# The fourth quarter of a unit's turned states: scaled by ScalarE, added up by an accumulating DMA from GpSimd

## The chip, the cores and the metric

The kernel runs on one core of one Trainium2 chip. The metric is the device time of one execution in microseconds; the kernel before was run three times, and its median counts. The engines are called as in the profile: PE (TensorE, matmuls and transposes), DVE (VectorE), ACT (ScalarE), POOL (GpSimd), SP (SyncE, which here only issues DMAs).

## What is computed

A Mamba-like mixer with a post layer norm, then a feed-forward layer with a routed low-rank part and a second layer norm, for 4 sequences of 512 rows of 1024, all in float32. The change lies in the state loop of the mixer. Cut to that:

```python
proj = hidden_states @ W_in.T                 # u and gate, 2048 channels each
u = silu(conv(u) + conv_b)
dt, Bm, Cm = split(u @ Wx.T)                  # N = 16 values of Bm and Cm a row
delta = softplus(rmsnorm(dt) @ Wdt.T + dt_bias)
def step(state, xs):                          # over the 512 rows
    dA = exp(d_t[..., None] * A)
    state = dA * state + (d_t * u_t)[..., None] * B_t[:, None, :]
    y_t = einsum('bdn,bn->bd', state, C_t)    # the sum over n
    return (state, y_t)
y = (ys + u * D_param) * silu(gate)
x = layernorm(x + y @ W_out.T)
x = layernorm(x + ffn(x))
```

## The kernel before

**Units.** The state loop is cut into 256 units (b, g, n): sequence b, a group g of 4 channel tiles (512 channels), and one of the 16 state values n. A group has 16 units, so the 16 groups (0 to 15 here, in the order of time) are 4 sequences times 4. A unit has these steps:

- POOL makes the drive, delta * u times the row B of this n, for 4 tiles at once (L1563, 128x2048), in one of 3 drive buffers.
- ACT makes the decay exp(delta * A) of each tile in PSUM (L1355), 4 a unit, 3 banks.
- DVE scans each tile (L1115), 4 a unit, in place in the drive buffer.
- PE turns the states (transposes, L933): turn (s, tt) puts the quarter tt of unit s, 128 of the 512 rows by 512 channels, into one of 2 PSUM banks, state_t. It needs the unit's last scan, and the reading of the quarter two turns before.
- Each of the 4 quarters is scaled by the value of C of its row, a scalar a partition, and added to y_acc (128 x 4 x 512 in SBUF). For n = 0 ACT writes it (first, L1366). For all other n there are two ways: DVE does both in one instruction (add, L1123), or ACT scales the quarter into the buffer scaled (L1375) and POOL adds that to y_acc (sum, L1568).

Behind n = 15 PE turns the sum back (y_turn), and DVE (y_skip) and POOL (y_gate) finish it. Beside this chain PE works off the products: the in products of the next sequence with weights split in a high and a low part (u_mm, g_mm, lines L964 to L966; the low part is made by POOL, w_low, L1588), the out products of this or the last one (o_mm, L987), and the feed-forward ones.

**What sets the order.** A planner (class Plan) plays the kernel through with a cost for each piece, and starts on each free engine the ready piece that is due first; every engine then runs its list in that order, with semaphore waits. put() gives a piece its engine, due time, cost, needs, and the buffers it takes and gives back. The two ways of a quarter are rivals there (either): whichever the planner can start first is done and the other struck out. The way over ACT is allowed only when POOL is free within FREE_IN = 3 us and has no work due more than DUE_EARLIER earlier. It chose the DVE way 727 times and the other 233 times: 8 times in group 0, 15 in group 1, and 12 to 18 in each later one, on any of the quarters (94 times the first, 26 the second, 82 the third, 31 the fourth). There is one scaled buffer, and there are 4 scratch buffers, which gates, copies and other rows share.

```python
put("DVE", i + 5 - ADD_FIRST, 0.645, "add", (s, tt), [*turned, summed(s - 1, tt)])
put("ACT", i + 5 - ADD_FIRST, 0.575, "scale", (s, tt), turned, take=[("scaled", (s, tt))], ahead_of="POOL")
put("POOL", q + 4, 1.23, "sum", (s, tt), [("scale", (s, tt)), summed(s - 1, tt)], give=[("scaled", (s, tt))])
plan.either(("add", (s, tt)), ("scale", (s, tt)))
```

Of the kernel before, what the change touches and what calls it, by code (L numbers as in the profile page):

```python
# [7 lines left out]
ALU = mybir.AluOpType  # L8
ACT = mybir.ActivationFunctionType
AX = mybir.AxisListType  # L10

P = 128
# [33 lines left out]
BANKS, SCRATCH, RAW, SPLIT = 3, 4, 4, 4  # L46
# [12 lines left out]
FREE_IN, DUE_EARLIER = 3, 8  # L59

def added(s, tt):

    if UNITS[s][2] == 0:
        return [(("first", (s, tt)), ("first", (s, tt)))]
    return [(("add", (s, tt)), ("add", (s, tt))), (("scale", (s, tt)), ("sum", (s, tt)))]
# [15 lines left out]
def any_of(names):  # L82
    return tuple(names) if len(names) > 1 else names[0]

def turn_read(s, tt):
    return any_of([read for read, _ in added(s, tt)])

def summed(s, tt):  # L90
    return any_of([end for _, end in added(s, tt)])
# [14 lines left out]
class Plan:  # L106
# [11 lines left out]
    DELAY = {"PE": 0.25, "DVE": 0.13, "ACT": 0.13, "POOL": 0.15, "SP": 2.0}  # L118

    def __init__(self):  # L120
        self.pieces, self.work = {}, {e: [] for e in ENGINES}
        self.count, self.total = {}, {}
        self.pools = {"bank": BANKS, "scratch": SCRATCH, "raw": RAW, "split": SPLIT, "dt": 1, "scaled": 1}
        self.place, self.before, self.prior, self.rival = {}, {}, {}, {}
        self.weights = []

    def put(self, engine, due, us, stage, key, needs=(), take=(), give=(), spare=0, kb=0, ahead_of=None):
# [5 lines left out]
                                       give=list(give), spare=spare, kb=kb, order=len(self.pieces), ahead_of=ahead_of)  # L133

    def either(self, add, scale):

        self.rival[add], self.rival[scale] = (scale, 2), (add, 1)

    def done_way(self, names):

        return next(name for name in ([names] if names in self.pieces else names) if name in self.count)

    def arrange(self):
# [6 lines left out]
        for name, piece in self.pieces.items():  # L150
            for need in set(piece["needs"]):
                left[name] += 1
                for way in [need] if need in self.pieces else need:
                    then[way].append(name)
# [12 lines left out]
        while finished < wanted:  # L167
            for e in ENGINES:
                for entry in sorted(ready[e]) if at[e] <= now else []:
# [4 lines left out]
                    on = piece["ahead_of"]  # L174
                    if on and (at[on] > now + FREE_IN or any(due < entry[0] - DUE_EARLIER for due, _, _ in ready[on])):
                        continue
                    ready[e].remove(entry)
                    if entry[2] in self.rival:
                        lost, pieces = self.rival[entry[2]]
                        wanted -= pieces  # L180
                        for other in ENGINES:
                            ready[other] = [x for x in ready[other] if x[2] != lost]
# [13 lines left out]
                    end = at[e] + self.DELAY[e]  # L196
# [28 lines left out]
def make_plan():  # L225
# [327 lines left out]
    for s, (b, g, n) in enumerate(UNITS):  # L553
# [13 lines left out]
        put("POOL", q - 8, 4.56 if s else 2.35, "drive", s, [("fetch", s), ("du", (b, g, 1))] + ([] if s else [("drive_begun", 0)]) + (  # L567
# [8 lines left out]
        for tt in range(TT):  # L576
            i = TT * s + tt
            turned = [("turn", (s, tt)), ("ssm_norm", b)]
            put("PE", i + 4 - TURN_FIRST, 0.45, "turn", (s, tt), [("scan", (s, GT - 1)), *([] if i else [("ssm_norm", 0)])] + (
# [1084 lines left out]
```

## Time and profile before

| | |
|---|---|
| Runs, us | 2257.61, 2262.97, 2263.51 (median 2262.97) |
| Span of the profiled execution, us | 2257.2 |
| Units of the state loop run, us from the start | 142 to 2136 |
| Mean granted PE clock, as a share of the full one | 0.964 |
| PE, DVE, POOL, ACT busy in the span | 91%, 88%, 81%, 66% |

The span goes from the first instruction's start to the last one's end. A time of the table's first row is of a whole execution; the lowest, 2257.61, is 0.4 us over the span of the profiled one. The busy time of an engine is the union of its instructions' times; an idle stretch ahead of an instruction is put down to what ended it. DVE's instructions overlap by about 0.08 us when one follows the other, so the distance of two starts is what one costs, not the duration. Group k starts with unit 16 k; the first scans of groups 2 and 12 stand at 426.0 and 1669.7 us.

### The profile page before, as it was taken

The page shows a single profiled execution, that of the slowest core. Times are in us where ns is not written, and L with a number is a line of the kernel's source. Part 1 is how long each engine was busy: PE and PEld are TensorE (multiplying, and loading weights), DVE is VectorE, ACT ScalarE, POOL GpSimd, SP SyncE. Part 2 cuts the span into 40 slices and gives each one's busy share as a digit, 9 for nine tenths or more (in the row PEclk, how much of TensorE's full clock was granted, in tenths as well). Part 3 has the DMA queues.
Part 4 walks back from the last instruction along what each step waited for, and adds up shares of the span by engine and source line. Part 5 has one row for each costly group of instructions (what it writes and reads, how often), then busy time and mean ns, then how long its engine had stood idle before and what let it go on. Part 6 is the DMA issues. An engine that isn't in the chain of part 4 may idle for free. (4 is left out here: it accounts for less than half of the span.)

```text
span 2257.2 us, 30761 instructions
## 1 busy us (share of the span) xinstructions
PE 2063.3 (91%) x10528; PEld 1562.5 (69%) x10528; DVE 1986.4 (88%) x2398; ACT 1486.3 (66%) x2198; POOL 1824.8 (81%) x786
## 2 busy tenths in 40 slices
PE   8989789889999799799998997989999998897998
PEld 6867577778565478687875555867875556785677
DVE  4447779999999999899999999999999999999943
ACT  4478658787666677666886657676786667756531
POOL 4279899998898889768799997979788998698840
PEclk9989899999999999999999998999999999998999
DMA  4466566665333447655463432475463337443340
GB/s 157 138 223 235 204 221 219 203 205 179 92 118 86 126 132 239 209 193 182 158 199 95 111 96 96 147 264 171 143 203 101 110 96 233 148 144 132 101 143 38
DMA packets 168764, 354.84 MB, mean 157 GB/s; under 512 B 18656, under 2 KB 45408, under 8 KB 168608
## 3 DMA queue, kind: packets, MB, share of 16 engines
q1 hardware_dynamic: 168608, 352.87, 48.6%
q8 instruction: 84, 1.38, 0.2%
q14 instruction: 72, 0.59, 0.1%
HBM read 283.96 MB, written 68.85 MB: 156 GB/s over the span
## 5 line engine op out<-in xcount | busy, mean ns | idle before, releaser
L1563 POOL TENSOR_TENSOR drive<-delta_u,b_bcast 128x2048 f32<-128x2048 f32 (+1 forms) x257 | 1172.5, 4564 | 129.1 <-PE state_t L933 120.6
L1115 DVE TENSOR_TENSOR_SCAN drive<-decay,drive 128x512 f32<-128x512 f32 x1024 | 1190.5, 1203 | 62.0 <-POOL drive L1563 37.9
L1355 ACT ACTIVATE decay<-delta,a_sb 128x512 f32<-128x512 f32 x1024 | 694.7, 688 | 377.9 <-DVE drive L1115 374.6
L933 PEld LDWEIGHTS state_t<-identity,drive 128*128 128x128 f32 x4096 | 492.0, 146 | 311.1 <-DVE drive L1115 141.8
L933 PE MATMUL state_t<-identity,drive 128*128 128x128 f32 x4096 | 591.1, 284 | 119.8 <-DVE drive L1115 95.1
L1123 DVE SCALAR_TENSOR_TENSOR y_acc<-state_t,c_rows,y_acc 128x512 f32<-128x512 f32 x727 | 515.3, 734 | 54.3 <-PE state_t L933 51.7
L964 PE MATMUL bank<-cols_high,w_split 128*128 128x512 f32 (+1 forms) x1240 | 524.4, 423 | 26.6 <-POOL w_split L1588 11.8
L966 PE MATMUL bank<-cols_high,w_split 128*128 128x512 f32 (+1 forms) x1240 | 491.8, 397 | 0.0
L965 PE MATMUL bank<-cols_low,w_split 128*128 128x512 f32 (+1 forms) x1240 | 489.6, 395 | 0.0
L987 PE MATMUL bank<-channels,w_raw 128*128 128x512 f32 x896 | 420.2, 596 | 2.3 <-DVE rows L1177 2.0
L1568 POOL TENSOR_TENSOR y_acc<-y_acc,scaled 128x512 f32<-128x512 f32 x233 | 300.1, 1288 | 102.2 <-ACT scaled L1375 101.9
L964 PEld LDWEIGHTS bank<-cols_high,w_split 128*128 128x128 f32 (+1 forms) x1240 | 236.3, 191 | 71.9 <-issue 16.2
L966 PEld LDWEIGHTS bank<-cols_high,w_split 128*128 128x128 f32 (+1 forms) x1240 | 234.8, 189 | 54.5 <-issue 0.2
L965 PEld LDWEIGHTS bank<-cols_low,w_split 128*128 128x128 f32 (+1 forms) x1240 | 237.1, 191 | 38.7 <-issue 0.5
L1588 POOL TENSOR_TENSOR w_split<-w_raw,w_split 128x512 fp32r<-128x512 f32 (+1 forms) x130 | 165.7, 1283 | 110.6 <-ACT w_split L1396 110.5
L987 PEld LDWEIGHTS bank<-channels,w_raw 128*128 128x128 f32 x896 | 156.4, 192 | 123.8 <-issue 121.3
L1375 ACT ACTIVATE scaled<-state_t,c_rows 128x512 f32<-128x512 f32 x233 | 159.2, 683 | 109.1 <-PE state_t L933 81.9
L1130 DVE SCALAR_TENSOR_TENSOR channels<-bank,conv_w_sb,channels 128x511 f32<-128x511 f32 (+2 forms) x192 | 142.7, 744 | 48.0 <-ACT channels L1404 43.5
L1396 ACT ACTIVATE w_split<-w_raw 128x512 fp32r<-128x512 f32 (+1 forms) x130 | 80.5, 621 | 58.9 <-PE bank L966 16.4
L1355 ACT ACT_TABLE_LOAD x80 | 102.6, 1283 | 2.0 <-DVE drive L1115 0.6
L1584 POOL TENSOR_TENSOR channels<-channels,scratch 128x512 f32<-128x512 f32 x64 | 81.5, 1296 | 12.3 <-DVE channels L1167 12.3
L1577 POOL TENSOR_TENSOR delta_u<-delta,channels 128x512 f32<-128x512 f32 x64 | 80.8, 1293 | 5.9 <-ACT delta L1458 5.5
(204 smaller groups left out, 1451.8 us busy)
## 6 DMA issues: line engine op xcount, KB each, us to landing
w_split<-w_split SPq DMA_DIRECT2D x272, 512.0 KB, 4.0
b_bcast<-b_rows SPq DMA_DIRECT2D x256, 256.0 KB, 3.4
w_raw<-in_w_out SPq DMA_DIRECT2D x112, 256.0 KB, 3.0
w_raw<-in_w_in SPq DMA_DIRECT2D x96, 256.0 KB, 4.1
gates<-scratch SPq DMA_DIRECT2D x64, 256.0 KB, 3.7
scratch<-gates SPq DMA_DIRECT2D x64, 256.0 KB, 4.7
rows<-in_x_rows SPq DMA_DIRECT2D x4, 2048.0 KB, 8.2
out<-rows SPq DMA_DIRECT2D x16, 512.0 KB, 4.8
```

Of the source, the lines that this page charges most:

```text
L933: last = engine.transpose(bank[0:tile.shape[1], i * P:(i + 1) * P], tile, identity[:, :])
L964: engine.matmul(bank[:, :], high[:, k % WK, :], cols_high[:, k, :], start=first, stop=False)
L965: engine.matmul(bank[:, :], high[:, k % WK, :], cols_low[:, k, :], start=False, stop=False)
L966: engine.matmul(bank[:, :], low[:, k % WK, :], cols_high[:, k, :], start=False, stop=last).then_inc(signal[stage])
L987: engine.matmul(bank[:, :], tile[:, k % WK, :], chan[s % 2][:, k, :], start=(k == tiles[0]), stop=(k == tiles[-1])).then_inc(signal["o_mm"])
L1115: engine.tensor_tensor_scan(state, decay[(GT * s + t) % DECAYS][:, :], state, 0.0, ALU.mult, ALU.add).then_inc(signal["scan"])
L1123: engine.scalar_tensor_tensor(y_acc[:, tt, :], bank[:, :], c, y_acc[:, tt, :], ALU.mult, ALU.add).then_inc(signal["add"])
L1355: engine.activation(decay[i % DECAYS][:, :], delta[:, g % 2, t, :], ACT.Exp, scale=a_sb[:, j, n:n + 1]).then_inc(signal["decay"])
L1375: engine.activation(scaled[:, :], bank[:, :], ACT.Copy, scale=c_rows[b % 2][:, tt, n:n + 1]).then_inc(signal["scale"])
L1563: engine.tensor_tensor(drive[key % DRIVES][:, tiles, :], du[:, tiles, :], row, ALU.mult).then_inc(signal[stage])
L1568: engine.tensor_tensor(y_acc[:, tt, :], y_acc[:, tt, :], scaled[:, :], ALU.add).then_inc(signal["sum"])
L1588: engine.tensor_tensor(pair[:, 1, 0:cols], raw[place["raw", key]][:, 0:cols], pair[:, 0, 0:cols].bitcast(F32), ALU.subtract).then_inc(sign ...
```

## The change

The choice between the two ways is fixed. The rivals, FREE_IN, DUE_EARLIER and ahead_of are gone from the planner. For the units with n from 1 to 14 the fourth quarter (tt = 3, BY_DMA) is scaled by ACT into one of 2 scaled buffers and added to y_acc by a DMA with accumulation, 128 x 512 float32 (256 KB), that POOL issues on its own queue; the planner counts 1.0 us for the issue and 4.0 us until it has landed. The three other quarters, and all four of n = 15, are DVE's adds. POOL waits, before it issues the DMA of a unit, until the DMA of the unit before has landed (both change the same rows of y_acc); the fourth add of n = 15 waits on DVE for the landing of n = 14. SCRATCH goes from 4 to 3. turn now waits for all four scans, drive for the drive before. The space for descriptors of DMAs issued by GpSimd goes from 64 to 512.

```diff
-BANKS, SCRATCH, RAW, SPLIT = 3, 4, 4, 4
+BANKS, SCRATCH, RAW, SPLIT, SCALED = 3, 3, 4, 4, 2
...
-FREE_IN, DUE_EARLIER = 3, 8
...
+BY_DMA = range(TT - 1, TT)
+
+
+def by_dma(s, tt):
+
+    return 0 < UNITS[s][2] < N - 1 and tt in BY_DMA
...
+    return "first" if UNITS[s][2] == 0 else "scale" if by_dma(s, tt) else "add", (s, tt)
...
+    return ("sum", s) if by_dma(s, tt) else turn_read(s, tt)
...
+    DMA_SUM = 4.0
...
-            put("DVE", i + 5 - ADD_FIRST, 0.645, "add", (s, tt), [*turned, summed(s - 1, tt)])
-            put("ACT", i + 5 - ADD_FIRST, 0.575, "scale", (s, tt), turned, take=[("scaled", (s, tt))], ahead_of="POOL")
-            put("POOL", q + 4, 1.23, "sum", (s, tt), [("scale", (s, tt)), summed(s - 1, tt)], give=[("scaled", (s, tt))])
-            plan.either(("add", (s, tt)), ("scale", (s, tt)))
+            if by_dma(s, tt):
+                put("ACT", i + 5 - ADD_FIRST, 0.575, "scale", (s, tt), turned, take=[("scaled", s)] if tt == BY_DMA[0] else [])
+            else:
+                put("DVE", i + 5 - ADD_FIRST, 0.645, "add", (s, tt), [*turned, summed(s - 1, tt)])
+        if by_dma(s, BY_DMA[0]):
+            put("POOL", q + 8, 1.0, "sum", s, [x for tt in BY_DMA for x in (("scale", (s, tt)), summed(s - 1, tt))], give=[("scaled", s)])
...
                 elif stage == "sum":
-                    s, tt = key
-                    e.wait_ge(*done("scale", key))
-                    e.wait_ge(*in_sum(s - 1, tt))
-                    engine.tensor_tensor(y_acc[:, tt, :], y_acc[:, tt, :], scaled[:, :], ALU.add).then_inc(signal["sum"])
+                    i = place["scaled", key]
+                    for tt in BY_DMA:
+                        e.wait_ge(*done("scale", (key, tt)))
+                        e.wait_ge(*in_sum(key - 1, tt))
+                    engine.dma_start(y_acc[:, BY_DMA[0]:BY_DMA[-1] + 1, :], scaled[i][:, :, :], accum_op=ALU.add).then_inc(sum_landed[i], 16)
...
-    nc = bacc.Bacc("TRN2", target_bir_lowering=False, num_devices=1, dynamic_dma_scratch_size=64)
+    nc = bacc.Bacc("TRN2", target_bir_lowering=False, num_devices=1, dynamic_dma_scratch_size=512)
```

The planner now makes another order on every engine. Adds and split quarters by group, from the two orders: before, 8 and 15 quarters went over ACT in groups 0 and 1 and 210 in groups 2 to 15; now 14 in every group.

POOL, from the drive of unit 188 on to the first drives of group 12 (unit 192 is drive0 behind the delta_u rows). Before:

```order
L1563 TENSOR_TENSOR drive2<-delta_u,b_bcast0 128x2048
L1568 TENSOR_TENSOR y_acc<-y_acc,scaled 128x512
L1563 TENSOR_TENSOR drive0<-delta_u,b_bcast1 128x2048
L1563 TENSOR_TENSOR drive1<-delta_u,b_bcast0 128x2048
L1568 TENSOR_TENSOR y_acc<-y_acc,scaled 128x512
L1563 TENSOR_TENSOR drive2<-delta_u,b_bcast1 128x2048
L1568 TENSOR_TENSOR y_acc<-y_acc,scaled 128x512
L1577 TENSOR_TENSOR delta_u<-delta,channels1 128x512 x4
L1563 TENSOR_TENSOR drive0<-delta_u,b_bcast0 128x2048
L1568 TENSOR_TENSOR y_acc<-y_acc,scaled 128x512
L1563 TENSOR_TENSOR drive1<-delta_u,b_bcast1 128x2048
```

and of the change (there L1554 is the drive, L1569 delta_u, L1560 the accumulating DMA):

```order
L1554 TENSOR_TENSOR drive2<-delta_u,b_bcast0 128x2048
L1560 DMA y_acc<-scaled0 128x512
L1554 TENSOR_TENSOR drive0<-delta_u,b_bcast1 128x2048
L1560 DMA y_acc<-scaled1 128x512
L1554 TENSOR_TENSOR drive1<-delta_u,b_bcast0 128x2048
L1560 DMA y_acc<-scaled0 128x512
L1554 TENSOR_TENSOR drive2<-delta_u,b_bcast1 128x2048
L1560 DMA y_acc<-scaled1 128x512
L1569 TENSOR_TENSOR delta_u<-delta,channels1 128x512 x4
L1560 DMA y_acc<-scaled0 128x512
L1554 TENSOR_TENSOR drive0<-delta_u,b_bcast0 128x2048
L1560 DMA y_acc<-scaled1 128x512
```

Where a sum stood at a place or not, by the planner's choice, a DMA stands behind each drive; the one behind drive0 is that of n = 14 of group 11, for which the fourth add of n = 15 waits.

DVE, in the same place: from the scans of unit 191 (drive2, n = 15) to those of unit 192 (drive0). The scans read a decay bank, the adds state_t0 (quarters 1 and 3) or state_t1 (2 and 4). Before:

```order
L1115 SCALAR_TENSOR_TENSOR drive2<-decay2,drive2 128x512
L1115 SCALAR_TENSOR_TENSOR drive2<-decay0,drive2 128x512
L1123 SCALAR_TENSOR_TENSOR y_acc<-state_t1,c_rows0,y_acc 128x512
L1115 SCALAR_TENSOR_TENSOR drive2<-decay1,drive2 128x512
L1123 SCALAR_TENSOR_TENSOR y_acc<-state_t0,c_rows0,y_acc 128x512
L1123 SCALAR_TENSOR_TENSOR y_acc<-state_t1,c_rows0,y_acc 128x512
L1115 SCALAR_TENSOR_TENSOR drive2<-decay2,drive2 128x512
L1115 SCALAR_TENSOR_TENSOR drive0<-decay0,drive0 128x512
L1115 SCALAR_TENSOR_TENSOR drive0<-decay1,drive0 128x512
L1123 SCALAR_TENSOR_TENSOR y_acc<-state_t0,c_rows0,y_acc 128x512
```

and of the change (L1106 the scan, L1114 the add), from the scan of unit 191's last tile on:

```order
L1106 SCALAR_TENSOR_TENSOR drive2<-decay2,drive2 128x512
L1106 SCALAR_TENSOR_TENSOR drive0<-decay0,drive0 128x512
L1114 SCALAR_TENSOR_TENSOR y_acc<-state_t0,c_rows0,y_acc 128x512
L1114 SCALAR_TENSOR_TENSOR y_acc<-state_t1,c_rows0,y_acc 128x512
L1106 SCALAR_TENSOR_TENSOR drive0<-decay1,drive0 128x512
L1114 SCALAR_TENSOR_TENSOR y_acc<-state_t0,c_rows0,y_acc 128x512
L1106 SCALAR_TENSOR_TENSOR drive0<-decay2,drive0 128x512
L1114 SCALAR_TENSOR_TENSOR y_acc<-state_t1,c_rows0,y_acc 128x512
L1106 SCALAR_TENSOR_TENSOR drive0<-decay0,drive0 128x512
```

Unit 191 has all its adds on DVE both times; the fourth one (the last L1114) now stands behind the third scan of unit 192. In the units before it, the quarter that leaves DVE was any one and is now always the fourth.

## Rows read from the trace of the kernel before

**Rows 1.** Page, parts 1 and 3: busy time, share, instructions; DMA packets, MB, share

```profile
PE 2063.3 (91%) x10528; PEld 1562.5 (69%) x10528; DVE 1986.4 (88%) x2398; ACT 1486.3 (66%) x2198; POOL 1824.8 (81%) x786
...
q1 hardware_dynamic: 168608, 352.87, 48.6%
```

**Rows 2.** Stretch, us; busy PE, PEld, DVE, ACT, POOL (instructions), clock, DMA share, GB/s

```profile
142.00:426.00 284.00, 248.40 (x1270) 200.16 (x1268) 234.56 (x258) 211.95 (x313) 261.54 (x122) 0.95 0.65 224
426.00:2136.00 1710.00, 1580.17 (x8184) 1170.84 (x8184) 1646.58 (x1957) 1176.24 (x1728) 1471.12 (x593) 0.97 0.48 151
```

**Rows 3.** Waits in 426 to 2136 us: us in total, times, longest

```profile
POOL drive L1563 <- PE state_t L933: 117.9, 81, 8.4
...
POOL y_acc L1568 <- ACT scaled L1375: 101.9, 66, 5.1
...
DVE y_acc L1123 <- PE state_t L933: 32.7, 45, 2.8
ACT scaled L1375 <- POOL y_acc L1568: 25.0, 29, 2.3
...
DVE drive L1115 <- ACT decay L1355: 18.6, 16, 3.1
...
PE state_t L933 <- ACT scaled L1375: 6.9, 11, 1.7
```

**Rows 4.** Waits in 142 to 426 us

```profile
DVE drive L1115 <- POOL drive L1563: 36.7, 11, 13.6
...
POOL w_split L1588 <- ACT w_split L1396: 14.8, 9, 3.9
```

**Rows 5.** Timeline of DVE: start, us, instruction, [idle before]

```profile
683.86 1.60 DVE L1123 SCALAR_TENSOR_TENSOR y_acc<-state_t,c_rows,y_acc 128x512 f32<-128x512 f32 x2 [1.21 <-PE state_t L933]
...
990.52 1.41 DVE L1123 SCALAR_TENSOR_TENSOR y_acc<-state_t,c_rows,y_acc 128x512 f32<-128x512 f32 x2 [1.24 <-PE state_t L933]
...
1673.27 1.21 DVE L1115 TENSOR_TENSOR_SCAN drive<-decay,drive 128x512 f32<-128x512 f32 x1
...
2023.47 0.72 DVE L1123 SCALAR_TENSOR_TENSOR y_acc<-state_t,c_rows,y_acc 128x512 f32<-128x512 f32 x1
2024.11 1.21 DVE L1115 TENSOR_TENSOR_SCAN drive<-decay,drive 128x512 f32<-128x512 f32 x1
...
2136.97 0.75 DVE L1123 SCALAR_TENSOR_TENSOR y_acc<-state_t,c_rows,y_acc 128x512 f32<-128x512 f32 x1 [0.75 <-PE state_t L933]
```

**Rows 6.** Groups of DVE in 426 to 2136 us: busy, mean ns, idle before

```profile
L1123 DVE SCALAR_TENSOR_TENSOR y_acc<-state_t,c_rows,y_acc 128x512 f32<-128x512 f32 x629 | 445.3, 733 | 34.8 <-PE state_t L933 32.7
```

**Rows 7.** Page, part 5: groups of POOL

```profile
L1563 POOL TENSOR_TENSOR drive<-delta_u,b_bcast 128x2048 f32<-128x2048 f32 (+1 forms) x257 | 1172.5, 4564 | 129.1 <-PE state_t L933 120.6
...
L1568 POOL TENSOR_TENSOR y_acc<-y_acc,scaled 128x512 f32<-128x512 f32 x233 | 300.1, 1288 | 102.2 <-ACT scaled L1375 101.9
```

**Rows 8.** Page, part 6: DMA issues, KB each, us to landing

```profile
w_split<-w_split SPq DMA_DIRECT2D x272, 512.0 KB, 4.0
...
gates<-scratch SPq DMA_DIRECT2D x64, 256.0 KB, 3.7
scratch<-gates SPq DMA_DIRECT2D x64, 256.0 KB, 4.7
```

**Rows 9.** Timeline of SP: one issue

```profile
1008.66 0.32 SPq L886 DMA_DIRECT2D b_bcast<-b_rows  x1
```

**Rows 10.** Timeline of POOL: first drives of groups 12 and 15

```profile
1665.07 4.61 POOL L1563 TENSOR_TENSOR drive<-delta_u,b_bcast 128x2048 f32<-128x2048 f32 x1
...
2013.29 4.65 POOL L1563 TENSOR_TENSOR drive<-delta_u,b_bcast 128x2048 f32<-128x2048 f32 x1
```

**Rows 11.** Busy us in a stretch of out products

```profile
570.00:627.00 57.00, 57.00 (x244) 32.92 (x243) 56.93 (x64) 32.48 (x51) 50.04 (x19) 1.00 0.35 96
```

**Rows 12.** Timeline of ACT ahead of a late decay

```profile
1370.26 4.62 ACT L1471 ACTIVATE rows<-rows,ln_shift,ln_rstd 128x1024 f32<-128x1024 f32 x4
1374.79 1.29 ACT L1355 ACTIVATE decay<-delta,a_sb 128x512 f32<-128x512 f32 x2
```

More of the change, by code:

```diff
@@ L122, in __init__, with put @@
         self.count, self.total = {}, {}
-        self.pools = {"bank": BANKS, "scratch": SCRATCH, "raw": RAW, "split": SPLIT, "dt": 1, "scaled": 1}
-        self.place, self.before, self.prior, self.rival = {}, {}, {}, {}
+        self.pools = {"bank": BANKS, "scratch": SCRATCH, "raw": RAW, "split": SPLIT, "dt": 1, "scaled": SCALED}
+        self.place, self.before, self.prior = {}, {}, {}
         self.weights = []
-    def put(self, engine, due, us, stage, key, needs=(), take=(), give=(), spare=0, kb=0, ahead_of=None):
+    def put(self, engine, due, us, stage, key, needs=(), take=(), give=(), spare=0, kb=0):
         assert (stage, key) not in self.pieces, (stage, key)
         self.pieces[stage, key] = dict(engine=engine, due=due, us=us, name=(stage, key), needs=list(needs), take=list(take),
[L133 to L141, printed above, removed]
+                                       give=list(give), spare=spare, kb=kb, order=len(self.pieces))
     def arrange(self):
@@ L152, in arrange @@
                 left[name] += 1
-                for way in [need] if need in self.pieces else need:
-                    then[way].append(name)
+                then[need].append(name)
             for what in piece["give"]:
@@ L641, in build_mixer_ffn @@
         scratch = [sbuf(f"scratch{i}", [P, T]) for i in range(SCRATCH)]
-        scaled = sbuf("scaled", [P, GT * P])
+        scaled = [sbuf(f"scaled{i}", [P, len(BY_DMA), GT * P]) for i in range(SCALED)]
         identity = sbuf("identity", [P, P])
@@ L762, in build_mixer_ffn @@
             landed[stage, key] = (to, raised[id(to)])
+        for _, stage, key in plan.work["POOL"]:
+            if stage == "sum":
+                to = sum_landed[place["scaled", key]]
+                raised[id(to)] = raised.get(id(to), 0) + 16
+                landed[stage, key] = (to, raised[id(to)])
         def read(s, tt):
-            return done(*plan.done_way(turn_read(s, tt)))
+            return done(*turn_read(s, tt))
         def in_sum(s, tt):
-            return done(*plan.done_way(summed(s, tt)))
+            return done(*summed(s, tt))
         def x_first(k):
@@ L940, in _ @@
                     s, tt = key
-                    e.wait_ge(*done("scan", (s, GT - 1)))
+                    for t in range(GT):
+                        e.wait_ge(*done("scan", (s, t)))
                     i = TT * s + tt
@@ L1369, in _ @@
                     b, g, n = UNITS[s]
[L1370 removed]
+                    bank, to, prior = state_banks[(TT * s + tt) % TURNED], scaled[place["scaled", s]], before["scaled", s]
                     e.wait_ge(*done("turn", key))
@@ L1374, in _ @@
                         e.wait_ge(*done(*prior))
-                    engine.activation(scaled[:, :], bank[:, :], ACT.Copy, scale=c_rows[b % 2][:, tt, n:n + 1]).then_inc(signal["scale"])
+                    engine.activation(to[:, tt - BY_DMA[0], :], bank[:, :], ACT.Copy, scale=c_rows[b % 2][:, tt, n:n + 1]).then_inc(signal["scale"])
                 elif stage == "x_high":
```

26 lines of the change are left out of this document (5 added, 21 removed).

## The prediction, made before the changed kernel was run

> **What bounds the kernel now.** I read the busy table first, then three stretches. Over the span PE is busy 91%, DVE 88%, POOL 81%, ACT 66% [rows 1], an average over stages with different limits. The second view splits it [rows 2]. In 426 to 2136 us, which holds groups 2 to 15 of the state loop, DVE is busy 1646.6 of 1710 us, so it stands idle for 63.4; PE is busy 1580.2, POOL 1471.1, ACT 1176.2. In 142 to 426 us (groups 0 and 1) the fullest engine is POOL, 261.5 of 284, and DVE has 234.6. The tail behind 2136 us has none of the work that the change touches. So DVE paces most of the kernel, PE close behind it, and POOL paces the start.
>
> The waits say the same. In the middle stretch DVE waits for PE's turns 32.7 us, for ACT's decays 18.6, and for POOL's drives only 1.2; POOL itself waits 117.9 us for turns before it may write a drive, that is, it runs ahead [rows 3]. In groups 0 and 1 DVE waits 36.7 us for POOL's drives [rows 4]. A reader should look there before the page's totals: taking 300 us off POOL is worth nothing in a stretch where nobody waits for POOL.
>
> **What the change takes from each engine.** Before, 727 adds are DVE's and 233 are split between ACT (scale) and POOL (sum). After, the split ones are the fourth quarter of units with n 1 to 14, 14 in each of 16 groups: 224. DVE has 736.
>
> *DVE.* Where the nine come from matters. By the order, groups 0 and 1 held 23 split adds and now hold 28; groups 2 to 15 held 210 and now hold 196. So in the stretch where DVE paces, it gains 14 adds. An add lasts 733 ns [rows 6], but neighbours overlap: two take 1.41 us, and a scan behind an add starts 0.64 after it [rows 5]; over the stretch I take 0.655 for one. 14 x 0.655 = **+9.2 us**. The 5 that DVE loses in groups 0 and 1 fall where it waits for POOL anyway: 0.
>
> *DVE's waits for turns.* A first add directly behind the unit's last scan must wait, since PE cannot turn before the scan ends: about 1.2 us each. In groups 2 to 15 the order has 12 such places, 14.5 us in all (the first at 683.86, one at 990.52, the last at 2136.97 [rows 5]); the new order has 17: 5 x 1.2 = +6.0. Against that, adds of the fourth quarter, and third-quarter adds behind a split one, now carry almost none of the rest of the 32.7 us; summed over the 629 adds of the stretch by what stands ahead of each, they carried about 9, and the new order keeps 2 of it. 6 - 7 = **-1 us**.
>
> *ACT.* Nine scales less, on an engine with 534 us idle in the middle stretch [rows 2]: 0.
>
> *POOL.* 233 sums at 1.288 us go (300.1 us [rows 7]), 224 DMA issues come. No row shows what GpSimd pays to issue one. The lower bound is SP's: 0.32 us an issue [rows 9]. The upper one is the drive, 4.56 [rows 7], the longest thing POOL does here. I take 1.1, since the instruction touches the same 128 rows as the sum at 1.29 does, without passing the data. In the middle stretch POOL has 239 us idle and gives back 271.7 for 196 issues, so it becomes the bound only if an issue costs over (239 + 272) / 196 = 2.6 us; 0 at 1.1. In groups 0 and 1 POOL paces: the order has 20 sums before the drive of unit 32, and the new one 27 issues, the other pieces being equal in number: 27 x 1.1 - 20 x 1.29 = 3.9, of which I count half, because POOL also stands 14.8 us for ACT there [rows 4]: **+2 us**. With 0.32 it would be -17 at full weight, with 2.6 +44.
>
> *The landing.* The new wait: POOL's issue for unit s waits until the DMA of unit s - 1 has landed, with later drives queued behind it; and at a group's end the fourth add of n = 15 waits on DVE for the landing of n = 14, with all later scans behind it, and PE's y_turn too. Mid-group a unit lasts about 7.6 us (1710 / 224), and a drive (4.6) stands between two issues, so a landing within some 6 us of its issue costs nothing. At the group's end the order puts the DMA behind the next group's first drive. In the trace such a drive ends at 1669.68 and 2017.94 [rows 10]. The third scan behind it ends at 1674.48 and the third add of its unit would follow, 5.4 us after the drive; at the other end the fourth add starts at 2023.47, 5.5 after it [rows 5]. Counted in the same way, nine of the fifteen ends have a margin between 4.3 and 6 us, the others up to 11. Transfers of 256 KB land in 3.7 to 4.7 us, of 512 KB in 4.0 [rows 8]; an accumulating one reads its target too. I take 4.1 behind an issue of 1.1, so 5.2: **+2 us** (9 x 0.2). Lower end 3.7, nothing; upper end 9 us, about twice the slowest median, below as a rival.
>
> The Trainium skill ("DMA: Bandwidth & Descriptors", anatomy of one DMA) gives about 2.0 us plus bytes / 436e3 for a DMA issued from GpSimd, 2.6 us here as an estimate. No row here shows such a DMA; the 256 KB rows are all longer. By that page the ends would cost nothing and the sum would be 2 us less.
>
> *The rest.* turn waits for all four scans instead of the last, drive for the drive before: DVE and POOL run in order, so 0. SCRATCH falls from 4 to 3, which could hold back PE's gate and out products; by the order PE has at least as much product work done by each group's start as before from unit 32 on, within 3 of about 5264 pieces where it is behind. 0, if DMAs land as they do now (stores of gates 3.7, loads 4.7 [rows 8]). More traffic: 224 x 0.26 MB is 59 MB on 353 [rows 1], so DMA share in the middle 0.48 [rows 2] becomes about 0.56, 0.64 if the second read counts fully.
>
> **The sum.** 9.2 - 1 + 2 + 2 = **+12 us**. The profiled execution has a span of 2257.2, and the run at 2257.61 is the one nearest to it; the other two are at 2263, and the median is 2262.97. So 2270 for an execution like the profiled one, and **2275** for the median.
>
> **Rivals.**
> 1. *The landing takes over* (slower still). One mechanism: accumulation makes the DMA long. From 5 us after the issue begins each further us costs about 9 us at the nine tight ends, from 6 on all fifteen, and from about 7.6, one unit, POOL's queue runs at the DMA's pace. At 8 us: 9 x 3 + 6 x 2 = 39 at the ends, over 2300. For: two reads and one write of 2 KB rows. Against: 512 KB lands in 4.0 [rows 8]. A milder form is contention.
> The Trainium skill (same page, "Issuing engines are not separate DMA queues") says DMAs of all issuing engines run on the same 16 DMA engines and interleave. By it the extra 59 MB also lengthens the weight loads; the DMA share, 0.65 in groups 0 and 1 against 0.48 later, says where that would begin. Its worth is in this case's 12%.
> 2. *The adds hide* (no change). In stretches of out products PE is busy 57.00 of 57 us with DVE at 56.93 [rows 11]. Groups 8 to 11 lie partly in such stretches, and 12 of the 14 adds fall in them. If it is PE that paces there, they go into DVE's 63 us of idle time: 9 us less, 2266 at the median, within 0.3%.
> 3. *Faster, by the banks.* Before, ACT's scale waits 25.0 us for POOL to free the one scaled buffer (29 times), POOL waits 101.9 us for scales with drives queued behind, and PE waits 6.9 us for ACT to free a state bank [rows 3]. With two buffers and a quarter that nobody on DVE follows, these go. If ACT's late decays (18.6 on DVE) came of them, and PE paces, the change gives back 6.9 + 18.6 and removes the 9.2: 2263 - 25 + 4 = about 2242; with half of it 2254. Against: a late decay such as that at 1374.79 stands behind four norms of 4.62 us, not behind a scale [rows 12]. It shows as faster once more than 11 of the 25 us are real.
> 4. *The change doesn't do what it says*: if POOL waits at the issue until the data has moved, an issue costs 3.7 or more [rows 8], over the 2.6 at which POOL paces: 2263 + 196 x 1.1 = above 2400. 2%, within the 12% of case 1.
>
> **The numbers.** Forecast 45% (own range 2266 to 2284), landing 12%, hidden 23%, faster 20%. A measurement of this kernel tells about 0.3%, 7 us, from no change. Of the forecast's 45 I count 39 as slower and 6 as same; of the hidden case 20 same, 3 faster; of the faster case 18 faster, 2 same; the landing case is slower. Faster 0.21, same 0.28, slower 0.51. The range leaves out half of the faster case and most of the landing case: 2249 to 2300.
>
> **What the new profile would show.** DVE's adds x736 at about 733 ns, DVE idle in the middle stretch still near 63 us and the stretch about 10 us longer: the forecast. DVE waiting at the group ends for a DMA, and PE's bank turns late there: rival 1. POOL's DMA rows over 2.6 us: rival 4. DVE idle well below 63 and the span unchanged: rival 2. ACT's scale without waits, DVE's wait for decays near zero and a shorter middle: rival 3. The forecast fails if POOL's issues are near 0.3 us, since then groups 0 and 1 gain up to 17 us, or if DVE's idle time moves by more than 10 us for reasons of order that a count of places does not catch.

## The result and the profile after

The changed kernel takes **2312.12 us** (median of 4 runs, 2305.58 to 2313.84), the kernel before 2263.24 beside it: a ratio of **1.0218, interval 1.0199 to 1.0238**, or 49 us slower. The forecast was 2275, with a range of 2249 to 2300: the sign was right and the size was not. The profiled executions have spans of 2310.4 and 2257.2 us.

First the page of the kernel after: busy time (to be held against [rows 1]), DMA queues, the chain that ended last, the groups of POOL ([rows 7]) and the landings ([rows 8]).

```profile
PE 2089.4 (90%) x10528; PEld 1573.2 (68%) x10528; DVE 1994.9 (86%) x2407; ACT 1479.6 (64%) x2189; POOL 1729.5 (75%) x777
...
q1 hardware_dynamic: 168608, 352.87, 47.5%
q0 software_dynamic: 32256, 58.73, 14.4%
...
PE 45%; DVE 23%; issue 9%; POOL 8%; ACT 7%; DMA 6%; SPq 0%; DVEq 0%; POOLq 0%; ACTq 0%
...
L1554 POOL TENSOR_TENSOR drive<-delta_u,b_bcast 128x2048 f32<-128x2048 f32 (+1 forms) x257 | 1201.2, 4690 | 269.4 <-PE state_t L923 255.4
...
L1560 POOL DMA_DIRECT2D y_acc<-scaled x224 | 207.8, 928 | 102.9 <-DMA y_acc<-scaled 63.0
...
L1580 POOL TENSOR_TENSOR w_split<-w_raw,w_split 128x512 fp32r<-128x512 f32 (+1 forms) x130 | 178.7, 1406 | 116.5 <-ACT w_split L1387 116.5
...
w_split<-w_split SPq DMA_DIRECT2D x272, 512.0 KB, 4.6
...
y_acc<-scaled POOLq DMA_DIRECT2D x224, 256.0 KB, 5.3
```

POOL has 95 us less work, as it should, and stands 63.0 us waiting for landings. Its drives, which nobody touched, have grown from 4564 to 4690 ns, and SP's 512 KB loads land in 4.6 us where they took 4.0. The DMA to y_acc is now 6% of the chain that ended last.

Then the stretches, with the columns of [rows 2]: the two that answer to it are groups 0 and 1, and groups 2 to 15.

```profile
143.00:437.00 294.00, 256.93 (x1285) 206.24 (x1284) 230.70 (x250) 216.52 (x320) 259.02 (x130) 0.93 0.77 241
437.00:2193.00 1756.00, 1601.31 (x8180) 1178.32 (x8179) 1660.11 (x1972) 1167.23 (x1716) 1383.28 (x581) 0.96 0.63 177
```

Groups 0 and 1 went from 284 to 294 us, groups 2 to 15 from 1710 to 1756. In the second stretch DVE's work grew by 13.5 us (1646.6 to 1660.1) and its idle time by 32.5 (63.4 to 95.9). The forecast had 9.2 of work there and 1 us of waits. The waits of that stretch, to be held against [rows 3] (us in total, times, longest):

```profile
POOL drive L1554 <- PE state_t L923: 248.6, 122, 7.1
...
ACT scaled L1366 <- PE state_t L923: 118.2, 78, 4.4
...
POOL y_acc L1560 <- DMA y_acc<-scaled: 51.3, 30, 4.9
DVE y_acc L1114 <- PE state_t L923: 36.3, 49, 2.9
DVE drive L1106 <- ACT decay L1346: 31.7, 27, 3.6
...
DVE y_acc L1114 <- DMA y_acc<-scaled: 7.3, 6, 2.5
...
DVE drive L1106 <- POOL drive L1554: 6.2, 4, 2.1
```

DVE's idle time grew in four places: decays 18.6 to 31.7, landings 0 to 7.3, POOL's drives 1.2 to 6.2, turns 32.7 to 36.3. That is 29.0 of the 32.5 us. Only one of the four names the DMA. How the DMA can reach DVE by way of another wait can be watched at one group end. POOL's timeline there (start, us, instruction, idle before):

```profile
1698.06 0.93 POOL L1560 DMA_DIRECT2D y_acc<-scaled  x1
...
1706.04 0.88 POOL L1560 DMA_DIRECT2D y_acc<-scaled  x1 [2.01 <-DMA y_acc<-scaled]
1706.64 4.91 POOL L1554 TENSOR_TENSOR drive<-delta_u,b_bcast 128x2048 f32<-128x2048 f32 x1
1713.00 0.90 POOL L1560 DMA_DIRECT2D y_acc<-scaled  x1 [1.45 <-DMA y_acc<-scaled]
```

and DVE's:

```profile
1711.58 1.22 DVE L1106 TENSOR_TENSOR_SCAN drive<-decay,drive 128x512 f32<-128x512 f32 x1 [1.24 <-POOL drive L1554]
...
1719.48 0.75 DVE L1114 SCALAR_TENSOR_TENSOR y_acc<-state_t,c_rows,y_acc 128x512 f32<-128x512 f32 x1 [2.47 <-DMA y_acc<-scaled]
```

POOL stands 2.01 us at 1706.04, until the DMA issued at 1698.06 has landed. The drive queued behind the issue starts that much later and ends at 1711.55, and DVE's scan, which stood 1.24 us, starts then. The next issue waits 1.45 us again, for the DMA issued at 1706.04, so that one took 7.0 us. The last one is issued at 1713.00 and holds DVE's fourth add until 1719.48, 6.5 us later. Three landings in a row hold this chain (8.0, 7.0 and 6.5 us behind their issues), and DVE pays at two places, 1.24 us for a drive and 2.47 for the landing itself.

### The profile page after: what moved, and what is told of

Same layout as the page of the kernel before. It is cut to its first block, busy times and chain, and to the rows that moved or that the text cites. A ratio compares the mean times of both kernels' runs of the same rounds, so it can differ in the third digit from the quotient of the medians.

```text
span 2310.4 us, 31004 instructions
## 1 busy us (share of the span) xinstructions
PE 2089.4 (90%) x10528; PEld 1573.2 (68%) x10528; DVE 1994.9 (86%) x2407; ACT 1479.6 (64%) x2189; POOL 1729.5 (75%) x777
## 3 DMA queue, kind: packets, MB, share of 16 engines
q0 software_dynamic: 32256, 58.73, 14.4%
## 4 chain that ended last, share of the span: by engine, by line
PE 45%; DVE 23%; issue 9%; POOL 8%; ACT 7%; DMA 6%; SPq 0%; DVEq 0%; POOLq 0%; ACTq 0%
DVE drive L1106 12%; PE bank L978 10%; PE state_t L923 10%; DVE y_acc L1114 6%; DMA y_acc<-scaled 6%; PE bank L955 5%; PE bank L957 5%; PE bank L956 5%; POOL drive L1554 5%; DVE channels L1121 2%; PE bank L923 2%; PE bank L1023 2%; POOL w_split L1580 1%; ACT decay L1346 1%; ACT L1346 1%
## 5 line engine op out<-in xcount | busy, mean ns | idle before, releaser
L1554 POOL TENSOR_TENSOR drive<-delta_u,b_bcast 128x2048 f32<-128x2048 f32 (+1 forms) x257 | 1201.2, 4690 | 269.4 <-PE state_t L923 255.4
L1106 DVE TENSOR_TENSOR_SCAN drive<-decay,drive 128x512 f32<-128x512 f32 x1024 | 1195.5, 1205 | 76.2 <-POOL drive L1554 38.3
L1114 DVE SCALAR_TENSOR_TENSOR y_acc<-state_t,c_rows,y_acc 128x512 f32<-128x512 f32 x736 | 523.1, 735 | 84.7 <-PE state_t L923 73.2
L955 PEld LDWEIGHTS bank<-cols_high,w_split 128*128 128x128 f32 (+1 forms) x1240 | 238.6, 192 | 75.1 <-issue 15.5
L1560 POOL DMA_DIRECT2D y_acc<-scaled x224 | 207.8, 928 | 102.9 <-DMA y_acc<-scaled 63.0
L957 PEld LDWEIGHTS bank<-cols_high,w_split 128*128 128x128 f32 (+1 forms) x1240 | 237.3, 191 | 55.5
L1580 POOL TENSOR_TENSOR w_split<-w_raw,w_split 128x512 fp32r<-128x512 f32 (+1 forms) x130 | 178.7, 1406 | 116.5 <-ACT w_split L1387 116.5
L1366 ACT ACTIVATE scaled<-state_t,c_rows 128x512 f32<-128x512 f32 x224 | 152.2, 679 | 136.7 <-PE state_t L923 123.4
L1569 POOL TENSOR_TENSOR delta_u<-delta,channels 128x512 f32<-128x512 f32 x64 | 85.9, 1577 | 5.6 <-ACT delta L1449 5.5
```

The source lines that it names most:

```text
L955: engine.matmul(bank[:, :], high[:, k % WK, :], cols_high[:, k, :], start=first, stop=False)
L957: engine.matmul(bank[:, :], low[:, k % WK, :], cols_high[:, k, :], start=False, stop=last).then_inc(signal[stage])
L1106: engine.tensor_tensor_scan(state, decay[(GT * s + t) % DECAYS][:, :], state, 0.0, ALU.mult, ALU.add).then_inc(signal["scan"])
L1114: engine.scalar_tensor_tensor(y_acc[:, tt, :], bank[:, :], c, y_acc[:, tt, :], ALU.mult, ALU.add).then_inc(signal["add"])
L1554: engine.tensor_tensor(drive[key % DRIVES][:, tiles, :], du[:, tiles, :], row, ALU.mult).then_inc(signal[stage])
L1560: engine.dma_start(y_acc[:, BY_DMA[0]:BY_DMA[-1] + 1, :], scaled[i][:, :, :], accum_op=ALU.add).then_inc(sum_landed[i], 16)
```

## The experiments

The theory after this profile: of the 49 us, part is the order that the new plan lays down, whatever carries out the sum, and part is the accumulating DMA. The rivals: the landing waits carry all of it; or the traffic does. Each ratio is to the kernel before, run beside it on the same chip.

**Who sums, in the same order.** Three kernels keep the changed order on every engine. The first lets POOL sum as it did before, the second leaves the fourth quarters' sums out, the third lets the DMA copy over y_acc in place of adding. The edits, shortened:

```diff
-engine.dma_start(y_acc[...], scaled[i][:, :, :], accum_op=ALU.add)
+engine.tensor_tensor(y_acc[:, TT - 1, :], y_acc[:, TT - 1, :], scaled[i][:, 0, :], ALU.add)   (e1)
+(nothing)                                                                              (e2)
+engine.dma_start(y_acc[...], scaled[i][:, :, :])                                       (e3)
```

> The changed kernel with one thing put back: POOL adds the scaled quarter to y_acc by its own instruction, at the place in its list where the DMA is issued. The order on all five engines is that of the changed kernel. Theory L (the landing costs: median 5.3 us from issue, 63 us of waits on POOL, 7 on DVE): the sum is done 1.3 us after it starts, the landing waits go, POOL's drives are back at 4.56 us; 2275, that is within 6 us of +12 over before. Theory O (the new order itself costs, whoever adds): it stays within 7 us of the changed kernel, 2305 to 2319.

> The changed kernel without the sum: POOL neither adds nor issues, so the fourth quarters of n 1 to 14 are left out of y_acc; ACT still scales them, and who waited for the sum waits for the scale. All other lists are the same. It is the floor for this order: Theory L: 2265 to 2275 (DVE has 14 adds more in groups 2 to 15 than before, and no landing). Theory O: 2300 or more. If it is under 2263, the sum's place on POOL matters more than DVE's adds.

> The changed kernel with a DMA that overwrites y_acc's fourth quarter in place of adding to it (the sum over n is lost for that quarter); same bytes written, same issue, same waits. It tells the price of accumulating. If the second read of the target makes the landing long: landing falls from 5.3 to about 4.2 us, POOL's waits for it from 63 to under 20, and the time to about 2290. If it is the path over GpSimd and not the accumulation: landing 5 us or more and 2305 to 2315.

Measured: e1 2288.58 us, ratio 1.0131 (1.0114 to 1.0148); e2 2277.19, 1.0082 (1.0067 to 1.0097); e3 2280.35, 1.0097 (1.0082 to 1.0113). So the changed kernel costs 18.6 us over the one before with no sum in it at all; nine more adds on DVE and the scratch buffer are in that number, beside the order itself. A plain copy adds 3 more, which these intervals do not tell from nothing, and accumulating adds 27 to that. POOL's own sum at the DMA's place (e1) costs 11 more than no sum and 8 more than the plain copy, so e1 lies between its two theories, 30 us over before, and the DMA costs 20 us more than the sum it stands for. e2 came out 2 us above the range of theory L, and e3 10 us under its 2290. POOL's groups and the landing in e3, the plain copy:

```profile
L1554 POOL TENSOR_TENSOR drive<-delta_u,b_bcast 128x2048 f32<-128x2048 f32 (+1 forms) x257 | 1170.1, 4554 | 340.0 <-PE state_t L923 319.3 <-DMA b_bcast<-b_rows 15.0 <-DMA y_acc<-scaled 3.6
...
L1560 POOL DMA_DIRECT2D y_acc<-scaled x224 | 129.9, 580 | 56.3 <-ACT scaled L1366 33.4 <-DMA y_acc<-scaled 15.2 <-PE state_t L923 5.8
...
q0 software_dynamic: 17920, 58.73, 6.6%
...
y_acc<-scaled POOLq DMA_DIRECT2D x224, 256.0 KB, 4.3
```

The same bytes need 80 packets a DMA and not 144, and 6.6% of the DMA engines' time and not 14.4%. They land in 4.3 us and not 5.3, are issued in 0.58 and not 0.93, and leave the drive at 4554 ns.

**The fixed choice by itself.** Here POOL sums again, and the planner is told so (1.23 us and POOL's own delay), with the choice fixed as in the change.

```diff
-put("POOL", q + 8, 1.0, "sum", s, ...)      end = ... DMA_SUM if stage == "sum"
+put("POOL", q + 4, 1.23, "sum", s, ...)     end = ... DELAY[e]
```

> The fixed choice with the sum on POOL and the planner told so (1.23 us, due as before, no landing of 4 us), so the order is made anew. It is the change without its DMA. Theory L: 2263 to 2275, the 14 adds of DVE in groups 2 to 15 being all that is left (9 us). Theory O in the form that a fixed choice is bad whatever follows: 2290 or more.

Measured: 2271.65 us, 1.0054 (1.0037 to 1.0072). Fixed choice, nine more adds and SCRATCH 3 together: 12 us, within the range of theory L. The kernel before with only the number SCRATCH set to 3:

> The kernel before with one number changed, SCRATCH 3 for 4, the planner's choice kept. It asks what the scratch buffer costs that the change gives up. If the buffer is not missed (as the prediction put it at 0): within 4 us of before. If it is part of the 18.6 us that the changed order costs even without any sum: 5 us slower or more.

2262.64 us, 1.0012 (1.0002 to 1.0022): 3 us. This is not the price of the buffer at equal work: with one buffer fewer the planner also chose the way over ACT 250 times and not 233, so DVE has 710 adds and not 727.

The order laid out for the DMA costs 6 us over one laid out for POOL when nobody sums (e2 against e4), and 17 when POOL sums in both (e1 against e4). The 6 do not lie in groups 2 to 15, which take 1734 us in e2 and 1732 in e4, but in groups 0 and 1, 285 against 276. What the order changes in groups 2 to 15 is for whom DVE waits. Its waits for decays there are 18.6 us before, 17.0 in e4, 27.8 in e2, 31.7 in the change. Two of the long ones, at the same places of the order: this is the timeline of DVE in e2,

```profile
531.44 3.59 DVE L1104 TENSOR_TENSOR_SCAN drive<-decay,drive 128x512 f32<-128x512 f32 x3 [3.57 <-ACT decay L1344]
1085.12 3.59 DVE L1104 TENSOR_TENSOR_SCAN drive<-decay,drive 128x512 f32<-128x512 f32 x3 [2.92 <-ACT decay L1344]
```

and this in the change, where the same scans wait as long:

```profile
542.35 3.59 DVE L1106 TENSOR_TENSOR_SCAN drive<-decay,drive 128x512 f32<-128x512 f32 x3 [3.57 <-ACT decay L1346]
...
1102.38 3.59 DVE L1106 TENSOR_TENSOR_SCAN drive<-decay,drive 128x512 f32<-128x512 f32 x3 [2.91 <-ACT decay L1346]
```

**Is it the wait or the work?** In e7 the DMA accumulates the scaled tile onto itself, so nobody needs its landing, except the scale that fills the slot again. The fourth quarters' sums are left out.

```diff
-engine.dma_start(y_acc[...], scaled[i][:, :, :], accum_op=ALU.add)
+engine.dma_start(scaled[i][:, :, :], scaled[i][:, :, :], accum_op=ALU.add)
```

> The order of the changed kernel; the accumulating DMA is issued as there, but from the scaled buffer onto itself, so y_acc misses the fourth quarters of n 1 to 14, and nobody waits for its landing except ACT, before it uses that buffer again two units later. It keeps the issue, the traffic and the work on POOL and takes the waits away. If the waits on the landing make the 27 us over the plain copy: 2278 to 2284, near the run without a sum. If it is what the accumulating DMA does to others while it runs (POOL's drives at 4.69 instead of 4.56 us, issues at 0.93 instead of 0.58, weights landing later): 2295 or more.

Measured: 2298.06 us, 1.0170 (1.0155 to 1.0185). That is 11 us less than the change; 16 us over the plain copy stay although POOL and DVE wait for no landing. The drive takes 4711 ns. But the waits for landings have not gone without a successor. A wait that is 3.0 us in the whole change, "issue", is 46.4 us here: POOL stands before the DMA with no semaphore to wait for.

```profile
POOL scaled L1561 <- issue: 46.4, 37, 3.7
```

```profile
300.05 1.00 POOL L1561 DMA_DIRECT2D scaled<-scaled  x1
300.66 5.05 POOL L1555 TENSOR_TENSOR drive<-delta_u,b_bcast 128x2048 f32<-128x2048 f32 x1
309.44 0.90 POOL L1561 DMA_DIRECT2D scaled<-scaled  x1 [3.73 <-issue]
```

Two reasons were open: the space for the DMA's descriptors is full, or the earlier DMA itself holds POOL. e9 is e7 with `dynamic_dma_scratch_size` 1024 in place of 512.

> As e7_dma_unwaited (accumulating DMA onto its own scaled tile, nobody waits for its landing but the next use of the slot, y_acc leaves out the fourth quarters), same order on every engine, only the space for POOL's DMA descriptors is doubled from 512 to 1024. In e7 POOL stood 46.4 us in 37 places before an issue with no semaphore to wait for, and the ratio was 1.017. Theory A, the space is full while the earlier accumulate is in flight: these 46 us go, and the time comes down from 2298 to 2280-2288. Theory B, the previous accumulating DMA or the engine itself holds the issue: the stalls stay at 35-55 us and the time within 4 us of 2298.

Measured: 2292.38 us, 1.0138 (1.0117 to 1.0158). The same place in e9:

```profile
300.02 0.76 POOL L1561 DMA_DIRECT2D scaled<-scaled  x1
300.63 4.79 POOL L1555 TENSOR_TENSOR drive<-delta_u,b_bcast 128x2048 f32<-128x2048 f32 x1
305.20 1.07 POOL L1561 DMA_DIRECT2D scaled<-scaled  x1
305.81 5.11 POOL L1555 TENSOR_TENSOR drive<-delta_u,b_bcast 128x2048 f32<-128x2048 f32 x1
```

**Bytes or number?** e12 is the change in its exact order, but a DMA covers 256 of the 512 columns; the other half of the fourth quarter's sum is left out.

```diff
-engine.dma_start(y_acc[:, BY_DMA[0]:BY_DMA[-1] + 1, :], scaled[i][:, :, :], ...)
+engine.dma_start(y_acc[:, TT - 1, 0:GT * P // 2], scaled[i][:, 0, 0:GT * P // 2], ...)
```

> The change in its exact order, but each accumulating DMA covers only the first half of the 512 columns (128 KB in place of 256 KB); the other half of the fourth quarter's sum is left out. Theory A, the cost of accumulating goes with bytes and packets in flight: landing 5.3 to 3.8-4.3 us, POOL's wait for landing 63 to under 20 us, drive 4.69 to 4.60 us, and the time is 2288-2296. Theory B, the cost goes with the issue or the mere number of accumulating DMAs: issue stays at 0.93 us, drive at 4.69, and the time stays at 2303-2312.

Measured: 2287.41 us, 1.0121 (1.0103 to 1.0139). Its POOL groups and DMA rows:

```profile
L1554 POOL TENSOR_TENSOR drive<-delta_u,b_bcast 128x2048 f32<-128x2048 f32 (+1 forms) x257 | 1201.5, 4693 | 282.6 <-PE state_t L923 266.1 <-DMA b_bcast<-b_rows 12.8 <-DMA y_acc<-scaled 3.2
L1560 POOL DMA_DIRECT2D y_acc<-scaled x224 | 210.2, 938 | 63.7 <-ACT scaled L1366 28.4 <-DMA y_acc<-scaled 22.6 <-PE state_t L923 8.5
...
q0 software_dynamic: 32256, 29.37, 8.3%
...
y_acc<-scaled POOLq DMA_DIRECT2D x224, 128.0 KB, 4.5
```

Both theories are half right, and the rows part them. The packets are as many as before, and so the issue (938 ns) and the drive (4693) stay. The landing falls from 5.3 to 4.5, POOL's wait for it from 63.0 to 22.6, and the time by 22 us. So what falls with the bytes is worth 22 us of the 49; the slower POOL and what else is left of the DMA cost the rest above e2, 9 us, and above the plain copy, whose drives are not slowed, 5.

**Would a plan that knows the landing help?** DMA_SUM is 4.0 us in the plan; the trace says 5.3 from issue start.

> The changed kernel with the planner told 7 us from issue to landing instead of 4, so that the fourth adds at the group ends and the issues stand later. If the landing costs because the plan counts on 4 us and gets 5.3 in the median and 7.3 in one of ten: 2285 to 2300, a good part of the 27 us between it and the plain copy comes back. If the cost is the wait itself (a drive queued behind on POOL, the whole group end held back): 2305 or more, and the ends get longer by what the plan adds.

> The change with DMA_SUM = 5.0 in place of 4.0 in its plan, near the measured landing of 5.3 us. Theory A, from e6_planned_7us (ratio 1.152, every unit 140-158 us per group): the planner can't place an issue of 1 us + landing behind a 4.56 us drive within one unit's 7.6 us, so the plan itself stretches; the plan's own length goes from 2257.7 to 2343 us, and the run adds about 50 us as in e6: 2380-2400. Theory B, the plan at 7.0 was a case by itself and a truer landing helps: the waits of 63 us on POOL fall under 30 and the time is 2290-2305.

Measured: with 7.0, 2604.87 us, 1.1520 (1.1500 to 1.1539); with 5.0, 2389.22, 1.0564 (1.0545 to 1.0584). The first is 300 us above the nearest number that its expectation named; "2305 or more" covers it by the letter only, for neither theory had a plan that stretches every unit. A theory of stretched plans made from that miss gave 2380 to 2400 for the second, and met it. The landing is as before (5.2 and 5.3 us); it is the order that spreads. DVE's waits in e11:

```profile
DVE y_acc L1114 <- PE state_t L923: 117.2, 110, 3.2
...
POOL y_acc L1560 <- DMA y_acc<-scaled: 57.5, 30, 5.2
...
DVE drive L1106 <- POOL drive L1554: 46.0, 29, 13.6
```

A planner that fills one engine at a time puts the issue (1.0), the landing (5.0) and a drive (4.56) that may have just begun in a row. That is 10.6 us on a chain with a pitch of 7.6, so it spaces units out in the plan, and the fixed order then keeps that spacing on the chip. That the chain is this one is my reading, and it is not complete: with 4.0 the same sum is 9.6, over the pitch too, and the plan spreads far less. That the spacing is the plan's is shown, since only the number in the plan differs.

**More for POOL instead.** e8 is e4 with n = 15 split too (240 sums, 720 adds on DVE):

> The replanned kernel with the sum on POOL, but n from 1 to 15 split instead of 1 to 14: 16 adds fewer on DVE (720), 240 sums on POOL. It tests the price of one add on the pacing engine: 16 x 0.655 = 10.5 us less than with 14 a group, if DVE paces, so about 2261, even with before, which has 727 adds. If other waits take it back: 2268 to 2275.

Measured: 2279.47 us, 1.0084 (1.0066 to 1.0101), 18 us above what was expected. DVE's idle time in groups 2 to 15 grew by 9.5 us over e4 and groups 0 and 1 by 10.3 (286.8 us, where e4 has 276.5 and the kernel before 284). A new order by itself moves the time by some 10 us, and a small saving in work can drown in it.

e10 keeps the choice of the kernel before and gives it a second scaled tile (the three settings, before and in e10):

```diff
-BANKS, SCRATCH, RAW, SPLIT = 3, 4, 4, 4        FREE_IN, DUE_EARLIER = 3, 8        "scaled": 1
+BANKS, SCRATCH, RAW, SPLIT = 3, 3, 4, 4        FREE_IN, DUE_EARLIER = 1, 8        "scaled": 2
```

> The kernel before, choice kept, with two scaled tiles in place of one (SCRATCH 3 to make room) and the planner's leeway for a scale set to 1 us in place of 3. POOL then sums 304 places in place of 233, DVE adds 71 fewer. Theory (my rival 3, ScalarE's 25 us of waiting for the one scaled tile is worth something): the wait ACT scaled<-POOL falls under 8 us, and the plan's own length, 12 us shorter than before's, comes through: 2244-2252, faster than both kernels. Rival: POOL, with 71 sums of 1.29 us = 92 us more, becomes late for the drives; DVE's wait for drive rises by over 15 us and the time is 2260-2275.

Measured: **2247.57 us, 0.9939 (0.9922 to 0.9956)**, as expected: 14 us faster than the kernel before and 64 faster than the change. Its busy time, its stretch of groups 2 to 15 and its wait for the scaled tile:

```profile
PE 2068.7 (92%) x10528; PEld 1570.8 (70%) x10528; DVE 1939.9 (86%) x2327; ACT 1521.6 (68%) x2267; POOL 1911.2 (85%) x857
```

```profile
419.00:2119.00 1700.00, 1579.01 (x8157) 1173.59 (x8156) 1605.33 (x1889) 1206.91 (x1788) 1553.38 (x660) 0.96 0.48 152
```

```profile
DVE drive L1117 <- POOL drive L1565: 39.8, 21, 13.6
...
ACT scaled L1377 <- POOL y_acc L1570: 8.6, 10, 2.1
```

ScalarE's wait is 8.6 us where it was 26.3, and DVE's wait for drives is 39.8, where it was 37.9: the rival did not come. But the gain is not the wait's own. DVE lost 71 adds, 41 us of work in groups 2 to 15 (1646.6 to 1605.3), and its idle time rose by 31, so that stretch is 10 us shorter; groups 0 and 1 are 9 us shorter (275 for 284). POOL takes 71 sums more, and that is the likeliest payer. SCRATCH 3 alone is e5, 3 us slower; the second tile and the leeway of 1 us were not tried apart.

## Why the prediction missed

The whole, laid out by the runs. "Over before" is the ratio times 2260 us. The stretches, and DVE's idle time in the second one, are of the one profiled execution of each, from the first scan to the first of group 2, and from there to the last add, 3 us later than in [rows 2].

| step | kernel | over before | groups 0, 1 | groups 2 to 15 | DVE idle there |
|---|---|---|---|---|---|
| the kernel before | before | 0 | 284 | 1713 | 65 |
| SCRATCH 3 (and 17 adds fewer) | e5 | +3 | 287 | 1719 | 77 |
| and the fixed choice, POOL sums | e4 | +12 | 276 | 1732 | 69 |
| and the order laid out for the DMA, no sum | e2 | +19 | 285 | 1734 | 74 |
| the same, POOL sums | e1 | +30 | 291 | 1740 | 80 |
| the same, a plain copy | e3 | +22 | 289 | 1735 | 75 |
| the same, half the bytes accumulated | e12 | +27 | 289 | 1737 | 77 |
| an accumulate whose landing POOL and DVE do not wait for, space 1024 | e9 | +31 | 292 | 1738 | 78 |
| the same, space 512 | e7 | +38 | 292 | 1744 | 83 |
| the change | after | +49 | 294 | 1760 | 97 |

Two terms of the sum failed. The larger is the landing, put at 2 us: accumulating costs 27 us over a plain copy in the same order, 18 of them for waiting. The smaller is the effect of the new order on DVE's waits, put at -1.

*DVE, +9.2.* Right. The stretch has 15 adds more (644 for 629) and 13.5 us more work, where 14 and 9.2 were forecast. What the adds cost by themselves no run shows: e4, with the fixed choice, has 19 us more in groups 2 to 15 and 8 less in groups 0 and 1.

*DVE's waits for turns, -1.* This step failed. The turns themselves moved by 3.6 us, and the 17 places came as counted, but the count asked only which add stands behind which scan. With no sum at all, e2's groups 2 to 15 take 1731 us against 1710, 10 of them beyond DVE's work:

```profile
428.00:2159.00 1731.00, 1591.92 (x8178) 1173.03 (x8177) 1657.23 (x1971) 1165.88 (x1714) 1212.74 (x383) 0.96 0.47 149
```

9 of those are waits for decays, whose places on ScalarE the new plan also set. I had named a drift of over 10 us "for reasons of order" as what would break the forecast, and gave it no width in the range; e8 shows that it is ordinary here.

*POOL's issue, 1.1 us.* Right: 0.93, and the next instruction starts 0.61 after it. What was missed is that an accumulating DMA also slows what POOL does meanwhile: the 64 drives that start within 0.7 us of an issue take 4.97 us in the mean, the 191 others 4.62, against 4.58 before. It costs little: e12 has drives as slow (4693 ns), e3 has them as fast as before (4554), and their stretches differ by 0 and 2 us, their times by 5. In groups 0 and 1, where POOL was to pace, the forecast had 2 us and the trace has 10: 1 with no sum, 5 with the plain copy or half the bytes. DVE does not wait longer for POOL's drives there (32.2 us for 36.7) but for turns (35.6 for 17.3, and 30.6 already in e2). So POOL's slower drives are not what lengthened them.

*The landing, 5.2 us.* The median is 5.3, almost the value taken, but the term built on it, +2, was mis-sized: taking the waits away gave 18 us (e9; 11 in e7, where stalls at the issue took their place), and halving the bytes 22 (e12). At the ends of groups 2 to 15 DVE waits 7.3 us in six places, in the whole kernel 9.2 in seven, about the upper end of 9. The error is the sentence that a landing within some 6 us costs nothing mid-group. It compared a median landing with a mean unit of 7.6 us. POOL's issues come when its queue lets them, one in four within 6.5 us of the one before, and landings scatter: one in four takes over 6.3 us, one in ten over 7.3. Nor does a drive always stand between two issues: in 17 of 223 pairs none does. One such place in the timeline of POOL in the change, where the landing holds the queue for 4.94 us although the issues would have been only 0.9 apart:

```profile
1546.85 0.90 POOL L1560 DMA_DIRECT2D y_acc<-scaled  x1 [0.41 <-ACT scaled L1366]
1552.69 0.87 POOL L1560 DMA_DIRECT2D y_acc<-scaled  x1 [4.94 <-DMA y_acc<-scaled]
```

*SCRATCH, 0.* 3 us in e5, with 17 adds fewer on DVE, so its own price may be higher; no run has it at equal work.

*The estimate of 2.6 us.* The prediction cited the Trainium skill ("DMA: Bandwidth & Descriptors", anatomy of one DMA) for an estimate of 2.6 us. The plain copy lands in 4.3 us here and the accumulating one in 5.3, so for the median the measurement decides against it; only the fastest of the 224 plain copies, at 2.3 us, comes down to it, with the DMA engines 56% busy in the mean of groups 2 to 15. The section "Issuing engines are not separate DMA queues" is borne out in direction: SP's 512 KB transfers land in 4.0 us before and in e1 and in 3.8 in e2, without DMAs from POOL, in 4.3 with the plain copies and in 4.6 with the accumulating ones.

*Rival 1* came at a landing of 5.3 us, at which it was priced at 2 or 3 us, and by way of POOL's queue more than by the ends. *Rival 2* fell: DVE's idle time rose. *Rival 3*: the waits it named mostly went (ScalarE's for its tile 26.3 to 12.5 us, now for landings; POOL's for scales 101.9 to 21.3; PE's for scales 7.9 to 1.2), but ScalarE's waits for turns rose from 81.9 to 123.4 us, and the decays came later, not earlier. *Rival 4* fell: 0.93 us an issue.

What stays open: how the 9 us between plain copy and unwaited accumulate with space 1024 divide between POOL's slower work (5 at most, by e12) and traffic, and whether the change itself gains from space 1024. PE's work in groups 2 to 15 also takes longer, 1601 us for 1580 at a granted clock of 0.96 for 0.97, and 1592 in e2; no run says whether that is a cause or a consequence of the longer stretch.

## What to carry to other kernels

A wait put into an in-order queue must be priced by the scatter of both sides, not median against mean: list the closest pairs, and count the instruction queued behind the wait and its consumer as well. Where a planner lays the order, first run the new order with the disputed operation left out; here that alone, with nine more adds in it, was 19 of 49 us, and the rest is what the operation costs. An estimate fed to a planner is not a measurement: setting it nearer the measured landing made this kernel 3.4% slower than leaving it low.

## What the hardware showed that I had not expected

Over the same 256 KB in SBUF, a DMA from GpSimd that accumulates takes 144 packets where a copy takes 80, an issue of 0.93 us against 0.58, a landing of 5.3 us against 4.3, and 14.4% of the DMA engines' time against 6.6%. With 128 KB the packets and the issue stay (144, 0.94 us) and the landing is 4.5.

GpSimd computes more slowly in a kernel that issues such DMAs, most of all directly behind an issue (4.97 us for the 128x2048 product): the 128x2048 product goes from 4554 to 4690 ns and the 128x512 one from 1287 to 1406, in the mean over all of them, also when nobody waits for the DMA. With a plain copy they keep their times.

A second accumulating DMA from GpSimd can stand up to 3.7 us at its issue with no semaphore in sight, 46.4 us in all (e7); doubling the descriptor space from 512 to 1024 removed all of it (e9).
